# Layer 2 attention: the context normed once, stored in device memory, and loaded normed four times

## What is computed

```python
cn = _ln(context, lnc_s, lnc_b)          # layer norm of each of the 1500 context rows
q = _ln(x, ln1_s, ln1_b) @ Wq            # 16 heads of 64
k, v = jnp.split(cn @ Wkv, 2, axis=-1)
k = jnp.concatenate((nk, k), axis=2)     # one null key and null value per head
v = jnp.concatenate((nv, v), axis=2)
sim = jnp.einsum('bhid,bhjd->bhij', q * 16 ** -0.5, k)
attn = jax.nn.softmax(jnp.where(mask, sim, max_neg), axis=-1)
out = jnp.einsum('bhij,bhjd->bhid', attn, v)
return _ln(out.reshape(b, n, 1024) @ Wo, lno_s, lno_b)
```

## Time and profile before

| | us |
|---|---|
| median of 3 runs | 2520.2 (2518.51 to 2523.51) |
| profiled execution | 2526.13 |
| its span, first to last instruction | 2524.3 |
| PE, DVE, ACT, POOL busy in the span | 2008.6, 1418.6, 1258.0, 1368.9 |

### The profile page before, as it was taken

How to read it: one execution, slowest core, us unless ns; L and a number is a source line. 1 busy time by engine, 2 the same in 40 slices (tenths; PEclk the granted TensorE clock), 3 DMA queues, 4 the chain that set the end, 5 groups by cost and what they waited for, 6 DMA issues and landing times. The chain is left out here.

```text
span 2524.3 us, 52181 instructions
## 1 busy us (share of the span) xinstructions
PE 2008.6 (80%) x21121; PEld 1411.6 (56%) x21121; DVE 1418.6 (56%) x2765; ACT 1258.0 (50%) x2169; POOL 1368.9 (54%) x1176
## 2 busy tenths in 40 slices
PE   6999999589979968766666665666686788999997
PEld 3777777468855546544444444444455445777774
DVE  5777776889835445433333333334350556777775
ACT  5777776357632255333333333333350146777773
POOL 7565651267729239777666666666666015443410
PEclk8999999689989879887887877878887888999998
DMA  5555442334321233222323322333310025444430
GB/s 159 149 143 150 134 132 69 88 105 141 92 54 40 82 106 93 79 77 76 88 77 88 88 87 78 89 89 89 89 50 25 17 80 145 137 138 135 141 93 9
DMA packets 105520, 240.03 MB, mean 95 GB/s; under 512 B 45689, under 2 KB 54929, under 8 KB 105025
## 3 DMA queue, kind: packets, MB, share of 16 engines
q1 hardware_dynamic: 105280, 236.69, 32.9%
HBM read 155.38 MB, written 0.65 MB: 62 GB/s over the span
## 5 line engine op out<-in xcount | busy, mean ns | idle before, releaser
L1615 PE MATMUL L2ps<-L2keys,L2qz 128*128 128x384 f32 x896 | 360.2, 549 | 330.5 <-DVE L2negmax L1806 329.8
L1707 POOL TENSOR_SCALAR L2values<-L2values,L2value_stats 128x127 f32<-128x127 f32 x768 | 617.1, 847 | 0.0
L1615 PEld LDWEIGHTS L2ps<-L2keys,L2qz 128*128 128x128 f32 x896 | 176.3, 207 | 474.9 <-DVE L2negmax L1806 336.9
L1631 PE MATMUL L2ps<-L2work,L2values 32*128 32x224 f32 x6144 | 334.5, 365 | 41.0 <-POOL L2values L1707 36.1
L1631 PEld LDWEIGHTS L2ps<-L2work,L2values 32*128 32x128 f32 x6144 | 295.4, 192 | 106.3 <-issue 58.8
L1816 DVE STREAM_TRANSPOSE L2work<-L2work 128x1568 f32<-128x1568 f32 x112 | 202.7, 1810 | 123.1 <-PE L2ps L1631 121.5
L1806 DVE CUSTOM_DVE_ANT_0 L2work<-L2ps,L2maskadd,L2big 128x1536 f32<-128x1536 f32 x112 | 203.6, 1818 | 119.1 <-PE L2ps L1615 119.1
L1744 ACT ACTIVATE L2work<-L2work,L2negmax 128x1536 f32<-128x1536 f32 x112 | 176.2, 1573 | 134.9 <-DVE L2negmax L1806 134.7
L1749 ACT ACTIVATE L2work<-L2work,L2rinv 128x1536 f32<-128x1536 f32 x112 | 176.8, 1579 | 116.9 <-DVE L2rinv L1821 116.9
L654 ACT ACTIVATE L3probsT<-L3ps 128x448 f32<-128x448 f32 x384 | 196.3, 547 | 72.5 <-PE L3ps L511 67.8
L654 ACT ACTIVATE L0probsT<-L0ps 128x448 f32<-128x448 f32 x384 | 198.3, 552 | 47.7 <-PE L0ps L511 46.7
(11 more groups left out here) (481 smaller groups left out, 4072.5 us busy)
## 6 DMA issues: line engine op xcount, KB each, us to landing
L2values<-in_ctx SPq DMA_DIRECT2D x192, 192.0 KB, 3.6
L0key_stack<-L0key_parts SPq DMA_DIRECT2D x192, 187.5 KB
L3key_stack<-L3key_parts SPq DMA_DIRECT2D x192, 187.5 KB
L0ctxT<-in_ctxT SPq DMA_DIRECT2D x16, 750.0 KB, 4.4
L1rawT<-in_ctxT SPq DMA_DIRECT2D x16, 750.0 KB, 6.6
L2mean_spread<-L_moments SPq DMA_DIRECT2D x16, 750.0 KB, 7.2
L3ctxT<-in_ctxT SPq DMA_DIRECT2D x16, 750.0 KB, 4.4
L2wqk<-L_moments SPq DMA_DIRECT2D x15, 750.0 KB, 27.1
```

The lines of the kernel that those rows point to most:

```text
L1615: last = nc.tensor.matmul(PS[:, score_bank(m) + w, 0:NCH * BW], tile_rows(m), key_window(b, w), start=True, stop=True)
L1631: last = nc.tensor.matmul(PS[:, 4 + a, 0:RT * BW], V[a * BW:(a + 1) * BW, n, :], block_cells(a, b, n), start=n == 0, stop=n == BLOCKS - 1, ...
L1707: last = nc.gpsimd.tensor_scalar(x, x, VST[:, 0, w, b, c:c + 1], VST[:, 1, w, b, c:c + 1], ALU.subtract, ALU.mult)
```

## The change

The four copies are no longer normed by POOL. For each batch, SP loads the context in its plain layout (125 partitions x 12 x 127 of 128 columns, `RAW`), POOL norms it with two broadcast instructions and `ctx_mv` (`normalise_values(b)`), SP stores it to a scratch tensor in device memory (`normal`), and the loads into the four partition groups read from there. PE waits for the loads directly. `VST`, the null column and their DMAs go; the null column is zero in `RAW` (set once) and the null rows are loaded as before. In SP's loop the store for batch b + 1 and the raw load for b + 2 stand between windows 1 and 2 of batch b. The raw buffer is single: a raw load waits for the store before it to have landed. The bias matmuls (L1670) get 128 equal columns in place of one.

```diff
@@ block.sync
+            def load_raw(b):
+                if b:
+                    sp.wait_ge(s.v_stored, 16 * b)
+                else:
+                    sp.wait_ge(s.v_zeroed, 2)
+                sp.dma_start(RAW[:, :, 0:P - 1], src["ctx"][b][:, :, 0:P - 1]).then_inc(s.raw_loaded, 16)
+
+            def store_values(b):
+                sp.wait_ge(s.v_ready, b + 1)
+                sp.dma_start(normal[b], RAW[:]).then_inc(s.v_stored, 16)
+
             def load_values(b, w):
+                sp.wait_ge(s.v_stored, 16 * (b + 1))
                 if b:
                     last_step = (NCH * w + NCH - 1) // RT
                     sp.wait_ge(s.pv_done, RT * (b - 1) + last_step + 1)
-                else:
-                    sp.wait_ge(s.v_zeroed, 1)
...
-                    sp.dma_start(V[a * BW:a * BW + n, w * NCH:(w + 1) * NCH, :], src["ctx"][b][w * BW:w * BW + n]
+                    sp.dma_start(V[a * BW:a * BW + n, w * NCH:(w + 1) * NCH, :], normal[b][w * BW:w * BW + n]
...
-            sp.wait_ge(ahead.s.means_ready, 1)
-            sp.wait_ge(ahead.s.spread, B)
-            sp.wait_ge(s.stats_zeroed, 1)
+            load_raw(0)
             sp.wait_ge(s.moments_stored, 16)
             load_moments(0)
-            for x, of in enumerate((ahead.means, rs)):
-                for w in range(WINDOWS):
-                    n = BW if w < WINDOWS - 1 else LAST_KEYS
-                    for a in range(4):
-                        sp.dma_start(VST[a * BW:a * BW + n, x, w], of[w * BW:w * BW + n]).then_inc(s.stats_spread, 16)
-            for w in range(WINDOWS):
-                load_values(0, w)
             for a in range(4):
                 at = a * BW + LAST_KEYS
                 sp.dma_start(V[at:at + 1, BLOCKS - 1, :], k.ident[P - 1:P, :]).then_inc(s.null_rows, 16)
-            for b in range(B):
+            load_keys(1)
+            store_values(0)
+            load_raw(1)
+            load_moments(1)
+            load_mask(1)
+            for w in range(WINDOWS):
+                load_values(0, w)
+            store_values(1)
+            load_raw(2)
+            for b in range(1, B):
                 if b + 1 < B:
                     load_keys(b + 1)
                     load_moments(b + 1)
                     load_mask(b + 1)
-                if b:
-                    for w in range(WINDOWS):
-                        load_values(b, w)
+                load_values(b, 0)
+                load_values(b, 1)
+                if b + 1 < B:
+                    store_values(b + 1)
+                if b + 2 < B:
+                    load_raw(b + 2)
+                load_values(b, 2)
+                load_values(b, 3)
@@ block.tensor
-                pe.wait_ge(s.v_ready, WINDOWS * b + blocks[-1] // NCH + 1)
+                for w in range(blocks[0] // NCH, blocks[-1] // NCH + 1):
+                    pe.wait_ge(values_loaded[w], 64 * (b + 1))
...
-                last = nc.tensor.matmul(PS[:, 4, 0:1], W[:, 3, h, :], U[:, 1, h:h + 1], start=h == 0, stop=h == H - 1)
+                last = nc.tensor.matmul(PS[:, 4, 0:P], W[:, 3, h, :], U[:, 1, h:h + 1].to_broadcast([HD, P]), start=h == 0, stop=h == H - 1)
@@ block.gpsimd
-            def normalise_values(b, w):
-                pool.wait_ge(values_loaded[w], 64 * (b + 1))
-                blocks = slice(w * NCH, (w + 1) * NCH)
-                nc.gpsimd.tensor_copy(V[:, blocks, P - 1:P], NULL[:, blocks].unsqueeze(2))
-                for c in range(NCH):
-                    x = V[:, w * NCH + c, 0:P - 1]
-                    last = nc.gpsimd.tensor_scalar(x, x, VST[:, 0, w, b, c:c + 1], VST[:, 1, w, b, c:c + 1],
-                                                   ALU.subtract, ALU.mult)
-                last.then_inc(s.v_ready, 1)
+            def normalise_values(b):
+                pool.wait_ge(s.raw_loaded, 16 * (b + 1))
+                x = RAW[:, :, 0:P - 1]
+                spread = lambda of: of.unsqueeze(2).to_broadcast([CH, NCH, P - 1])
+                nc.gpsimd.tensor_tensor(x, x, spread(k.ctx_mv[:, b, :, 0]), ALU.subtract).then_inc(s.v_centred, 1)
+                pool.wait_ge(s.v_centred, b + 1)
+                nc.gpsimd.tensor_tensor(x, x, spread(rs[:, b, :]), ALU.mult).then_inc(s.v_ready, 1)
...
-            nc.gpsimd.memset(VST[:, :, WINDOWS - 1], 0.0).then_inc(s.stats_zeroed, 1)
+            nc.gpsimd.memset(RAW[:, :, P - 1:P], 0.0).then_inc(s.v_zeroed, 1)
...
             normalise_keys(0)
-            pool.wait_ge(s.stats_spread, 16 * 2 * WINDOWS * 4)
-            pool.wait_ge(s.null_column, 2)
-            pool.wait_ge(s.null_rows, 64)
-            for b in range(B):
-                if b + 1 < B:
-                    normalise_keys(b + 1)
-                for w in range(WINDOWS):
-                    normalise_values(b, w)
+            normalise_values(0)
+            for b in range(1, B):
+                normalise_keys(b)
+                normalise_values(b)
             ln_pool(pool, k, s2)
```

More of the change, by code:

```diff
@@ L1408 @@
 class WideAhead:
-    SEMS = "w_loaded rows_loaded products scaled centred summed means_ready ve_ready spread"
+    SEMS = "w_loaded rows_loaded products scaled centred summed ve_ready spread"
     def __init__(self, ctx, nc, k, src):
@@ L1424, in __init__ @@
         self.rs = sb("rs", [CH, B, NCH])
-        self.means = sb("means", [CH, B, NCH])
         self.W = self.WORK[0:HD, 0:4 * H * P].rearrange("p (m h n) -> p m h n", m=4, h=H)
@@ L1457, in variances @@
     def variances(self):
-        self.nc.vector.tensor_copy(self.means[:], self.k.ctx_mv[:, :, :, 0]).then_inc(self.s.means_ready, 1)
         self.nc.vector.tensor_scalar(self.rs[:], self.k.ctx_mv[:, :, :, 1], 1e-6, None, ALU.add).then_inc(self.s.ve_ready, 1)
@@ L1484, in attention_16_wide_heads @@
         s = semaphores(ctx, nc, name, LN_SEMS + " folded_q folded_q_ready folded_v folded_v_ready bias_filled bias_ready q_filled q_act q_dve "
-                       "values_loaded0 values_loaded1 values_loaded2 values_loaded3 mask_loaded null_rows null_column constants margins mask_ready "
-                       "v_zeroed stats_zeroed stats_spread v_ready moments_filled moments_ready moments_stored slot_ready keys_loaded0 keys_loaded1 spread_loaded keys_moved keys_scaled "
+                       "values_loaded0 values_loaded1 values_loaded2 values_loaded3 mask_loaded raw_loaded null_rows constants margins mask_ready "
+                       "v_zeroed v_centred v_ready v_stored moments_filled moments_ready moments_stored slot_ready keys_loaded0 keys_loaded1 spread_loaded keys_moved keys_scaled "
                        "scores_filled max_done exp_done rinv_ready scaled turned pv_done heads_ready out_filled out_ready dve_chain")
@@ L1496, in attention_16_wide_heads @@
         V = sb("values", [P, BLOCKS, P])
-        NULL = sb("null_column", [P, BLOCKS])
-        VST = sb("value_stats", [P, 2, WINDOWS, B, NCH])
+        RAW = sb("raw", [CH, NCH, P])
         KEYS = sb("keys", [P, 2 * KEY_COLUMNS + (WINDOWS - 1) * BW - 3])
@@ L1503, in attention_16_wide_heads @@
         scratch = nc.dram_tensor("L2_moments", [2, B, NCH, CH], F32).ap()
+        normal = nc.dram_tensor("L2_normal_context", [B, CH, NCH, P], F32).ap()
         nmax = sb("negmax", [P, 4])
@@ L1823, in _ @@
             ln_dve(dve, k, s, PS, link, [1e-5, 1e-6], k.v("L2_1s"), k.v("L2_1b"))
[L1824 to L1827, removed]
             for h in range(H):
```

## The result

The changed kernel takes 2616.8 us (median of four runs, 2612.4 to 2622.2) against 2521.7 for the kernel before on the same chip: a ratio of 1.0379 [1.0355, 1.0404]. The forecast was 2617, in a range of 2540 to 2720. The agreement to 0.2 us is partly luck. The profiled execution after took 2612.4 us, the fastest of its four, so between the two profiles there are 86.3 us where the sum had 97; and the profile of before, on which that sum stands, was 0.24% above its median.

A forecast was written before the change was run, and what follows sets the result against it. The prediction took the late mask, queued behind window 3's loads on one DMA engine, as the bound. Head and 13 periods of 74.8 us gave +118, the tail -21: +97 on 2526.1, 2623, or 2617 us as a median; range 2540 to 2720.

The forecast's parts named there:

- The late mask: Layer 2's attention: ACT waits 344.5 us, 13 times, for the mask, holding up DVE and PE; masks 66.6 us apart.
- the rival of 2150: POOL was the bound: relieved, PE's 40 us a batch set the pace, 14 periods lose 26.6 each; chance 0.04.
- w3: The four 29-row loads of window 3, ahead of the mask in SP's queue: 28.4 us on one DMA engine.
- 125 rows on five engines: Store and raw load of 125 rows run on five DMA engines, 25 rows each, window 3's engine among them.
- The rival of all engines: 125-row transfers spread over all 16 engines, or avoid window 3's and don't hold SP: period 66.6, about 2485; chance 0.12.
- One engine (3500): 125-row transfers go on one engine: store 31 us, raw load 50, period up some 72, about 3500; chance 0.04.
- low bounds (12.2 and 8.3): After the mask lands, POOL's values ready at 12.8 us, at least 12.2; store 6.1 us plus 2.2 of latency.
- +8.2: Growth of the steady period between masks, from 66.6 to 74.8 us; 70.4 to 83.9 with all bounds on one side.
- as if issued at 33.0 rather than 24.8: Window 3's effective issue, in us after the mask's landing, delayed by raw load and window 2 on its engine.
- Head and tail: Head: batch 2's mask lands about 971, the last at 1943 against 1825.66, +118 us; tail: -21 us.
- the 9.8 that were to go twice: Tail: PE waits twice until POOL has normed window 3, 9.8 us after its landing; both waits go.
- the factor of two that the prediction tried: Raw load's 508-byte pieces at twice 20 ns: it would take 12.2 us, and the forecast would rise some 37 us.

The follow-up runs named there:

- e4: Kernel before with the mask of batch b+2 issued after the second window of batch b's values, ahead of the third and fourth: 2409.4 us, ratio 0.9552.
- e2: Kernel before with each of window 3's four 29-row loads issued as 16 and 13 rows: 2205.3 us, ratio 0.8747.
- e6: Changed kernel with the raw load taking whole rows of 128 columns (6144-byte pieces), POOL zeroing column 127 again: 2591.5 us, ratio 1.0271.
- e12: Changed kernel with the raw load of batch b+2 issued behind window 3 instead of ahead of window 2: 2591.0 us, ratio 1.0268.
- e1: Changed kernel with the store and the raw load each issued as 112 and 13 rows instead of 125: 2491.0 us, ratio 0.9884.
- e9: Changed kernel with window 3's loads issued as 16 and 13 rows, store and raw load as 112 and 13: 2120.5 us, ratio 0.8414.
- e7: Changed kernel with window 3's loads as 16 and 13 rows, store and raw load as 112 and 13, raw load in whole 128-column rows: 2112.9 us, ratio 0.8383.

## Why the prediction was right, point by point

- *The late mask is the bound, and POOL is not.* Shown: POOL waits 807.6 us now and the kernel got slower (the rival of 2150 falls); moving the mask alone (e4) or spreading w3 alone (e2) made the kernel before faster by 114 and 315 us.
- *w3's engine.* Shown by e2, and by shares of 0.06 and 0.07 in the traces of before, after, e6 and e12.
- *125 rows on five engines, w3's among them.* Shown: 0.31 during the store, and e12's four and one. By the rule that the prediction cites from the Trainium skill (DMA: Bandwidth & Descriptors, "Why a DMA increments its semaphore by 16 and not by 1") it is 16, 1 and 5 engines for 32, 29 and 125 rows; the traces agree: up to 1.01 while 32-row loads run (e6, with the raw load), 0.07 and 0.31. The rival of all engines was worked out at 2485; e1, which makes it true, takes 2491.0. One engine (3500) falls.
- *Sizes.* POOL's four operations: 2.73 to 2.84 us each, not 3.1, so the store goes out at 10.95 and not 12.8. The store: 7.5 to the raw load's issue, not 8.3. A raw piece: 7.3 us / 300 = 24 ns, not 33. All were priced too high, and the first two lie even under their low bounds (12.2 and 8.3). With the measured prices the sum's own steps have w3 move as if issued at 27.7, not 33.0; measured is 31.3. The other 3.6 us are not in the sum and were not taken apart in full. By these prices the raw load and window 2 were to be off the engines 10.4 us after the raw load's issue (8.4 and 2.0); but they slow each other down, and the raw load's last piece alone comes 11.8 us after its issue. Errors of 5.3 us one way and 3.6 the other offset each other, so that the period came out at +7.4 for +8.2 is partly luck.
- *Where the 7.4 lies.* The step "as if issued at 33.0 rather than 24.8" is right in kind, a queue on w3's engine, and near in size: 1.9 us before w3's issue and 4.6 behind it in the period shown, 31.3 in place of 33.0.
- *Head and tail.* Batch 1's mask at 913.4 with 3.15 us of waiting (about 911 and none), batch 2's at 976.3 (971), the last one +111.5 us (+118). The tail is -22.2 (-21): the way to the first group of it is 10.2 us shorter and the way on to the last 12.3, near the 9.8 that were to go twice, and the first group took 5.20 us (5.5). The idle ahead of the last group stays. Stage: +89.3, forecast +97.

## What to carry to other kernels

Before relieving the engine with the most busy time, ask which wait ends last: taking 536 us of work off POOL (1368.9 to 832.4 us busy) cost 95 us, because its round trip stood on the one DMA engine whose 28 us set the pace. Spread over more engines it gained 29 us with that engine left as it was (e1), and 85 us once w3 was spread too (e9 against e2). Look at the DMA share while each transfer runs: 0.07 or 0.31 where others show 0.75 is a transfer on one or five of 16 engines, and all that is queued behind it waits; splitting it into a multiple of 16 rows and the rest (29 as 16 and 13, 125 as 112 and 13) is a line of code. And a new transfer is paid for where it stands in the loop that the late one closes: the same edit of the mask was worth 114 us in the kernel before and 15 in the kernel after.

## What the runs showed of the hardware

- Pieces of 508 bytes: 102 GB/s in the raw load at a share of 0.34, against 124 at 0.31 and 0.32 for pieces of 6144 bytes on five engines; on one engine 21 GB/s against 28. That is a fifth to a quarter slower. The Trainium skill (DMA: Bandwidth & Descriptors, "Specifications") says that pieces under 512 bytes miss line rate, and these rows agree; the factor of two that the prediction tried is not what they show. e9 and e7, with small and with large pieces, differ by 0.4% at the same period.
- Which transfers meet counts for more than how many engines are busy: five moved 25 GB/s each; 16 moved 11 each while window 2 met the raw load (after, 1371 to 1375; e6, 1358 to 1361) and 22 each while keys and moments moved (e6, 1382 to 1385). Why was not tested.
- Issues can hold SP: 5.91 us at window 2 in the kernel after, behind the 1500 pieces of the raw load, and 22.21 us at the keys in e12. It isn't the small pieces alone: with 125 pieces (e6) window 2 went out without it, but w3's fourth load was held for 7.70 us, and in the kernel before the first key load behind w3 was held for 7.07. In e6 and e12 w3 goes out at its floor, and the period is only 1.4 and 2.2 us shorter, so the hold ahead of w3 was not the main loss.
